# Edge pass over eight heads: the sums of the first four blocks of the preceding group are added between the steps of this group's running maxima

## The reference

```python
for r in range(2):
    mask = edge_type == REL_EDGE_TYPE[r]
    score = jnp.sum(q_dst * k_r[src], axis=-1) * p_rel[r] * scale
    score = jnp.where(mask[:, None], score, -jnp.inf)
    m = jax.ops.segment_max(score, dst, num_segments=n)
    e = jnp.where(mask[:, None], jnp.exp(score - m[dst]), 0.0)
    den = jax.ops.segment_sum(e, dst, num_segments=n)
    alpha = e / jnp.where(den[dst] > 0, den[dst], 1.0)
    out = out + jax.ops.segment_sum(v_r[src] * alpha[..., None], dst, num_segments=n)
```

## Time and profile before

| what | us |
|---|---|
| median of 3 runs | 10689.3 |
| lowest and highest of the 3 | 10685.61 and 10701.63 |
| span of the profiled execution, first to last instruction | 10683.5 |
| pass with heads, first gather used to last sum added | about 6935 to 8212 |

### The profile page before, as it was taken

The page is one execution under the profiler, slowest core; times in us unless marked ns, Lnnn a source line. Parts: engine busy times, 40 slices in busy tenths (PEclk is TensorE's granted clock), DMA queues, the critical chain, the costliest instruction groups (busy, mean ns, idle before and its releaser), DMA issues. The chain is left out here.

```text
span 10683.5 us, 91403 instructions
## 1 busy us (share of the span) xinstructions
PE 3393.1 (32%) x16349; PEld 2854.6 (27%) x16350; DVE 4930.0 (46%) x14493; ACT 2459.5 (23%) x7194; POOL 6924.5 (65%) x7153
## 2 busy tenths in 40 slices
PE   3013222322243332423342222534444123242223
PEld 2001110222242222322232222423333123232223
DVE  4944443255554555455545555578887211121111
ACT  0300000122232222322232222244443222220000
POOL 0137777577767777577757777266664677737775
PEclk9995555566666666666676666766666566666666
DMA  2020000122222222122212222133332222212222
GB/s 30 8 45 2 2 2 4 36 53 54 54 44 52 53 54 53 42 54 53 53 42 53 54 54 50 55 91 89 89 90 59 76 53 53 53 44 53 53 53 53
DMA packets 367820, 524.23 MB, mean 49 GB/s; under 512 B 230148, under 2 KB 246958, under 8 KB 367322
## 3 DMA queue, kind: packets, MB, share of 16 engines
q0 software_dynamic: 244288, 480.25, 17.9%
q1 hardware_dynamic: 111424, 39.55, 1.8%
q10 hardware_dynamic: 11994, 3.15, 0.3%
HBM read 473.04 MB, written 49.42 MB: 49 GB/s over the span
## 5 line engine op out<-in xcount | busy, mean ns | idle before, releaser
L1176 POOL DMA_INDIRECT rows<-table_d,meta x3328 | 3188.3, 958 | 1111.6 <-issue 1003.3
L1196 PE MATMUL ps_total<-weighted_rows,ident 128*128 128x129 f32 (+1 forms) x8320 | 1776.4, 395 | 3778.7 <-ACT weighted_rows L1215 1572.1
L1196 PEld LDWEIGHTS ps_total<-weighted_rows,ident 128*128 128x128 f32 x8320 | 1599.0, 276 | 3956.5 <-ACT weighted_rows L1215 3071.6
L1281 DVE TENSOR_TENSOR prod<-rows,q_rows 128x258 f32<-128x258 f32 x1664 | 624.6, 424 | 1391.4 <-DMA rows<-table_d,meta 875.9
L1176 POOL DMA_INDIRECT rows<-pairs_d,meta x832 | 814.1, 979 | 446.3 <-issue 240.4
L1215 ACT ACTIVATE weighted_rows<-rows,corr 128x129 f32<-128x129 f32 x3328 | 998.8, 389 | 6.7
L976 POOL DMA_INDIRECT list_out_d<-tile_rec,tile_idx x784 | 799.8, 1020 | 254.4 <-issue 246.9
L1036 POOL DMA_INDIRECT tile_rows<-rows_d,tile_meta x833 | 785.9, 943 | 264.6 <-issue 253.3
L1036 POOL DMA_INDIRECT tile_rows<-table_d,tile_meta x833 | 785.8, 943 | 264.4 <-issue 253.3
L1045 DVE TENSOR_TENSOR sums<-sums,tile_sums 128x129 f32<-128x129 f32 x98 | 28.4, 290 | 1823.7 <-PE tile_sums L1086 1823.7
L1242 DVE SCALAR_TENSOR_TENSOR sums<-sums,corr,ps_total 128x129 f32 x1696 | 593.8, 350 | 412.9 <-DVE sums L1242 181.6
(11 more groups left out here) (469 smaller groups left out, 5818.9 us busy)
## 6 DMA issues: line engine op xcount, KB each, us to landing
rows<-table_d,meta POOLq DMA_INDIRECT x3328, 2.5
tile_rows<-table_d,tile_meta POOLq DMA_INDIRECT x833, 2.5
tile_rows<-rows_d,tile_meta POOLq DMA_INDIRECT x833, 2.5
rows<-pairs_d,meta POOLq DMA_INDIRECT x832, 2.8
list_out_d<-tile_rec,tile_idx POOLq DMA_INDIRECT x784, 2.1
meta<-list_in_d SPq DMA_DIRECT2D x260, 32.0 KB
tiles<-tiles_in_d SPq DMA_DIRECT2D x260, 0.0 KB
table_d<-h_rows,perm_in POOLq DMA_INDIRECT x245, 2.2
```

The costliest lines, as they stand in the source:

```text
L1176: pool.indirect_dma_start(rows[q][:, j, 0:width], None, table_d, bass.IndirectOffsetOnAxis(meta[q][:, j, number:number + 1], 0)).then_inc( ...
L1196: mm = pe.matmul(total[:, b, 0:W], k.ident[:], wide[:, j % WS, :], start=(j == b * J), stop=(j == b * J + J - 1))
L1281: own(dve.tensor_tensor(prod[:, js, :], rows[q][:, js, :], k.q[:, ds(tk[b], 1), :].to_broadcast([P, J, P + 1]), ALU.mult))
```

## The change

In the pass with heads, the wait for PE moves from behind the exponents to the front of the running maxima. Each of the first four steps of the maxima gets, between its copy and its minimum, the multiplication of one block of `add_sums`, and behind its minimum the addition of that block; a wait for all but the last instruction stands where a wait for all stood. `add_sums` itself then starts at block 4. Nothing changes in how often each instruction is executed. `add_sums` now begins with a wait for all of DVE's own instructions, in both modes.

Two bounds are read again from memory once their loop has ended instead of being held in a register: the number of iterations at the end of each edge pass (on DVE), and the number of steps at the end of one stage of the sorting (`place_edges`, on POOL).

```diff
@@ place_edges, after POOL's loop
+                ended = pool.value_load(plan[0:1, 1:2], min_val=1, max_val=NCH // G2)
                 for q in range(2):
-                    pool.wait_ge(scat[q], 16 + steps * CH * 16)
+                    pool.wait_ge(scat[q], 16 + ended * CH * 16)
@@ edge_pass, DVE
-                    def add_sums(own, q, tk):
-
-                        for b in range(B):
-                            a = k.acc[:, ds(tk[b], 1), 0:W].rearrange("p a w -> p (a w)")
+                    def keep_sum(own, q, tile, b):
+                        kh = kept[:].rearrange("p (r d) -> p r d", d=D_HEAD + 1)
+                        a = k.acc[:, ds(tile, 1), 0:W].rearrange("p a (r d) -> p (a r) d", d=D_HEAD + 1)
+                        own(dve.tensor_tensor(kh, a, corr[q][:, S + b, :].unsqueeze(2).to_broadcast([P, R, D_HEAD + 1]), ALU.mult))
+
+                    def add_sum(own, tile, b):
+                        a = k.acc[:, ds(tile, 1), 0:W].rearrange("p a w -> p (a w)")
+                        own(dve.tensor_tensor(a, kept[:], total[:, b, 0:W], ALU.add))
+
+                    def add_sums(own, q, tk, first=0):
+                        own.wait()
+                        for b in range(first, B):
                             if mode == "attend":
+                                a = k.acc[:, ds(tk[b], 1), 0:W].rearrange("p a w -> p (a w)")
                                 own(dve.scalar_tensor_tensor(a, a, corr[q][:, S + b, :], total[:, b, 0:W], ALU.mult, ALU.add))
                             else:
-                                kh = kept[:].rearrange("p (r d) -> p r d", d=D_HEAD + 1)
-                                own(dve.tensor_tensor(kh, a.rearrange("p (r d) -> p r d", d=D_HEAD + 1),
-                                                      corr[q][:, S + b, :].unsqueeze(2).to_broadcast([P, R, D_HEAD + 1]), ALU.mult))
+                                keep_sum(own, q, tk[b], b)
                                 own.wait()
-                                own(dve.tensor_tensor(a, kept[:], total[:, b, 0:W], ALU.add))
+                                add_sum(own, tk[b], b)
                             own.wait()
                         dve.sem_inc(m["sum_taken"], 1)
...
+                            back_tiles = late if q == 0 else before
+                            if mode == "heads":
+                                dve.wait_ge(m["block_summed"], (i * 2 + q) * B + (B // 2 + 1))
                             for b in range(B):
                                 running = k.nm[:, ds(tk[b], 1), 0:R].rearrange("p a r -> p (a r)")
                                 own(dve.tensor_copy(nmo[:, b, :], running))
-                                own(dve.tensor_tensor(running, running, nmb[:, b, :], ALU.min))
-                                own.wait()
+                                if mode == "heads" and b < B // 2:
+                                    if b:
+                                        own.wait(1)
+                                    keep_sum(own, 1 - q, back_tiles[b], b)
+                                    own(dve.tensor_tensor(running, running, nmb[:, b, :], ALU.min))
+                                    own.wait(1)
+                                    add_sum(own, back_tiles[b], b)
+                                    own.wait(1)
+                                else:
+                                    own(dve.tensor_tensor(running, running, nmb[:, b, :], ALU.min))
+                                    own.wait()
...
-                            if mode == "heads":
-                                dve.wait_ge(m["block_summed"], (i * 2 + q) * B + (B // 2 + 1))
-                            else:
+                            if mode != "heads":
                                 dve.wait_ge(m["summed"], i * 2 + (q + 2))
-                            add_sums(own, 1 - q, late if q == 0 else before)
+                            add_sums(own, 1 - q, back_tiles, B // 2 if mode == "heads" else 0)
...
@@ edge_pass, DVE, after the loop
-                    own = Steps(dve, m["own"], pairs * (2 * PER + 1))
+                    ended = dve.value_load(sched[0:1, ds(e, 1)], min_val=1, max_val=EPOCH)
+                    own = Steps(dve, m["own"], ended * (2 * PER + 1))
                     if mode == "heads":
-                        dve.wait_ge(m["block_summed"], pairs * (2 * B) + (B // 2 + 1))
+                        dve.wait_ge(m["block_summed"], ended * (2 * B) + (B // 2 + 1))
                     else:
-                        dve.wait_ge(m["summed"], pairs * 2 + 2)
+                        dve.wait_ge(m["summed"], ended * 2 + 2)
```

## The result

The changed kernel takes 10804.8 us at the median of four executions, the kernel before 10693.6 us. The ratio is 1.0108 with a 95% interval of 1.0095 to 1.0121. Taken again later it was 10792.6 against 10695.4 us, 1.0092 (1.0078 to 1.0106). The change costs 97 to 111 us. The prediction was slower, 10836 us, with a range of 10800 to 10900. The first time lies in it, 5 us above its lower end; the second, 10792.6 us, lies 7 us under it.

The account below looks back on a forecast made before the run. DVE is busiest, with PE's burst end a shoulder of the path; the moved wait exposes it. 53.14 + 0.40 - 47.79 = 5.75 us a pair, over 25.5 pairs 147; 10683.5 + 147, plus 5.8: 10836 us, range 10800 to 10900.

Parts of the forecast that it names:

- The count of the wait and its place: DVE's moved wait asks for all eight blocks of PE's preceding burst, idling DVE 5.4 and 3.6 us before the maxima.
- the rival on slow bursts: In the pass with heads, PE's longer pause makes all bursts long: 34 us more, 10870 us; chance 0.07.
- The cycle: One group's cycle in the pass with heads: 26.64 us (q = 1) and 26.50 us (q = 0), a pair 53.14 instead of 47.79.
- the work behind the wait: DVE's maxima, exponents, sums and weighting following PE's totals: 14.56 and 15.31 us, plus 0.40 a pair for interleaved steps.
- The second address: Accumulator address arithmetic repeated for L1248 behind a wait: taken at 0; as a rival 1.66 us a pair, 10878 us, chance 0.14.
- The rule of the Trainium skill: On DVE, the next operation starts only once the pipe is empty, and waits between cost nothing; sum would lie 59 us higher.
- The rival that went with the rule: Copy and minimum fill no gap in the four interleaved steps: 0.29 us each, 59 us, 10895 us; chance 0.11.
- What was costed at nothing: SP's list loads, POOL's longer wait (some 6 us), `powered`, `sum_taken`, the load of `ended` and the `add_sums` wait: no added time.
- the expected gain: Four plain steps of the maxima on DVE, 0.40 us each, saved in each group: 3.2 us a pair.
- The four hidden steps: Copy and minimum of four interleaved maxima steps on DVE counted at nothing, then 0.05 us each, 0.4 us a pair.

Follow-up runs that it names:

- e11: Changed kernel with only its wait made to fit: first four sums wait for their own totals, last four for all eight; 10628.1 us against 10715.7 before.
- e6: Changed kernel with full waits for all of DVE's own instructions in the interleaved steps (run matched by text order); 10882.3 us against 10695.4 before.
- e5: Changed kernel with all eight sums interleaved, each waiting for its own total (run matched by text order); 10587.1 us against 10695.4 before.

## Why the prediction was right

**The count of the wait and its place.** Right, and shown twice: the first copy starts 0.16 us behind PE's last matmul, in all 51 groups, and with waits that fit the idle time is gone. The idle time of DVE was forecast at 230 us and is 231.0. That it agrees so closely is luck: the two kinds of group have 5.0 and 4.1 us, where the forecast had 5.4 and 3.6. The reason is that PE's end does move; the prediction's sum held it fixed and left its moving to the rival on slow bursts. The bursts still last 9.5 to 10.7 us and still start 1.47 to 1.49 us into the cycle. With q = 1 they became shorter on average, 9.84 for 10.44 us, at a mean granted clock of 0.78 for 0.72; with q = 0 they became longer, 9.88 for 9.64 us, at 0.79 for 0.84. The two shifts partly cancel.

**The cycle.** The direction and the wait were right, the size came out near the edge of the range: 111 and 97 us more, where 147 was forecast. The cycles were forecast at 26.64 and 26.50 us and 0.4 for the steps of a pair, and measured 25.51 and 26.37. The exponents end 7.3 and 6.7 us later in the cycle than before, where about 8 was forecast. The pair is 1.66 us shorter than the sum had it, which is the 42 us between 147 and 105. The term that was mis-sized is the work behind the wait: 14.56 + 15.31 + 0.40 = 30.27 us forecast, 14.04 + 14.85 = 28.89 measured. Of the difference, the four interleaved steps make about 0.8: I took a plain block of sums plus 0.05 us and a lead of 0.1, and they last 1.03 and 1.14 us, no more than a block alone (1.05 and 1.17), with nothing for the copy and the minimum. The four plain steps make 0.35, since half of eight steps was more than four of them take (1.42 and 1.46 us for 1.60 and 1.63 in the groups shown). The start of the next sum behind L1343 makes 0.24 (0.35 and 0.42 us of idle time, where 0.51 and 0.52 were taken). The other 0.28 us is PE: its bursts let DVE start at 11.47 and 11.52 us instead of 12.08 and 11.19.

**The second address.** Taken at nothing, rightly. The arithmetic stands in front of L1241 alone, 8 times a group as before; L1245 has none:

```profile
L1241 DVEq FUSED_REGOPS  x8: 121/151/190, 7373.8 to 7384.6; - x8
```

**The rule of the Trainium skill** ("VectorE: DVE Perf Modes", The DRAIN you can't avoid), as the prediction uses it, would have made the copy and the minimum full price, and waits free. The prediction gives only a part of what stands there: the same paragraph goes on that a next operation which is not held starts earlier. The overlap agrees with that clause: the copy starts 0.36 us after an addition of 0.44 us. What the section says of waits, that a semaphore behind each of eight copies cost nothing, does not carry over to this order: exchanging loose waits for full ones costs 0.44 us a step. The rival that went with the rule has fallen.

**What was costed at nothing.** POOL's wait grew to 5.7 us (forecast about 6). POOL did not wait for the lists of edges in the first profile of the changed kernel, and once, for 0.3 us, in the second. The load of the bound shows no cost where it was tried alone. The rounds with one head take 4587.5 us in the first profile and 4578.9 in the second, 4581.7 before: no change.

**Where the expected gain went.** The four hidden steps are real: with q = 1 the eight steps of the maxima and four blocks of sums took 7.37 us (3.19 and 4.18) and now take 5.60, with q = 0 7.8 and now 6.0: 1.8 us a group, 91 us in all. The moved wait costs 231 us of idle time in place of 31. The difference of the two, 200 - 91 = 109 us, comes within 6 us of the loss of 103 to 104 us.

## What to carry to other kernels

Before moving work earlier on an engine, look at what the waits in front of it count, and not only at what the work needs: here the wait for eight sums, moved forward with four of them, held DVE for 4 to 5 us a group, and fitting the waits turned +104 into -85 us in the pass. Short independent instructions put between dependent long ones were free here only as long as the waits between them left the newest instruction open. When the first engine gets faster, ask for the next one at once: interleaving all eight brought 23 us instead of 82, because gathers and an uncovered exponential took over.

## What the runs showed of the hardware

On two chips all loops of this kernel took longer, with instructions of the same length: 13549 for 10690 us, 6467 for 4580 us in the four rounds, 1870 for 1284 in the pass with heads, with a stop of some 12 us on DVE's sequencer in nearly every group, at a place that moves with the waits. Why is not shown. A change of waits for which 9 to 31 us were expected elsewhere was worth 144 us there.

The last linear stage ran at another granted clock from execution to execution. The stretch behind the last gather, 223 matmuls each time, took 60.7 and 61.8 us at a mean clock of 0.81, 67.1 us at 0.73 (`e11`), 68.6 us at 0.70 (`e6`), 78.4 us at 0.57 (`e5`) and 80.8 us at 0.54. So single profiles of this kernel can differ by 20 us in code that no change touched.
